# A recommender tower on one core: two transfers moved in the DMA queue of SyncE

## The chip, the core and the metric

The kernel runs on one core of one Trainium2 chip. Its work is spread over five engines with an instruction stream each: TensorE (PE, matmuls into PSUM), VectorE (DVE), ScalarE (ACT), GpSimd (POOL) and SyncE (SP, which here only issues DMAs and waits). They order themselves by semaphores. The metric is the device time of one execution in microseconds; the kernel before takes 625.06 us (median of three runs, 624.83 to 626.06).

## The reference

For 1024 samples, 32 rows of 16 floats are gathered from 32 embedding tables. Three layers follow, in which every feature of the layer before is multiplied with every original row and contracted with weights; the sums over the 16 dimensions go with 16 dense inputs through a top network of three matrices.

```python
def _L0_rec_ref(embeddings, W0, W1, W2):
    x0 = embeddings
    xk = x0
    outs = []
    for W in (W0, W1, W2):
        xk = jax.nn.relu(jnp.einsum('bmd,bhd,mhk->bkd', x0, xk, W))
        outs.append(jnp.sum(xk, axis=2))
    return jnp.concatenate(outs, axis=1)
e = jnp.stack([tbl_0[ids[:, 0]], ...], axis=1)
z = _L0_rec_ref(e, L0_rec_W0, L0_rec_W1, L0_rec_W2)
h = jnp.concatenate([z, dense_ctx], axis=1)
h = jnp.maximum(h @ W_top1 + b_top1, 0.0)
h = jnp.maximum(h @ W_top2 + b_top2, 0.0)
y = h @ W_top3
```

## The kernel before, in words

The 1024 samples are worked in 16 steps of 64 samples; a step is 1024 columns (64 samples x 16 dimensions) wide. All in f32. Steps are numbered from 0 here, so "step 1" is the second.

A step's data goes through these stages:

1. **Gather.** POOL issues 16 indirect DMAs (line 291) that bring the step's rows into `emb` (two buffers, even and odd steps). The gathers of steps 0 and 1 stand at POOL's start; those of step s + 2 are spread behind POOL's six products of step s (1, 1 and 8 behind the three of layer 1, then 1, 1 and 4 behind the three of layer 2).
2. **Store.** When the last of them has landed, SP stores `emb` to a scratch tensor in HBM, `x0_rows` (`store_rows`, line 236, two DMAs, 192 KB).
3. **Load.** When the store has landed, SP loads `x0g` (`load_x0g`, line 246, 512 KB) and then sixteen tiles `x0bc` (`load_tiles`, line 263, 512 KB each). The tiles live in a ring of 24 slots, so the first eight of a step can be loaded early and the other eight wait until tiles of the step before have been used in its layer 2.
4. **Layers.** DVE multiplies pairs of tiles with the layer's input (line 336), PE contracts the products with weights (line 518). Layer 0 uses tiles 0 to 3 in two DVE instructions; layers 1 and 2 use all sixteen, of which DVE takes tiles 0 to 12 in eight instructions (seven groups, the first in two halves) and POOL tiles 13 to 15 (line 306; 11 to 15 or 12 to 15 in the last two steps). POOL's tile k of a layer goes to PE before DVE's group 2, 3 and 5. DVE's products have a ring of 4, POOL's too.
5. **ACT** moves PE's result to the next layer's input for DVE (`x_ps`, line 418) and for POOL (`x_sb`, line 435), and makes the layer sums.

On DVE and PE the order is: layer 1 of step s, layer 0 of step s + 1, layer 2 of step s. The weights of the top network (seven DMAs on SP, line 278: 256, 160, 512 and 64 KB and three of 1 or 2 KB) are first waited for by PE in step 4. Arrivals of tiles are counted by one semaphore per pair of tiles (`bc_in[g]`), so a reader of tile 14 waits for tile 15 as well.

What sets the order around the change is the order of SP's program: SP issues strictly in turn, and a wait holds all that stands behind it. `x0bc` of step 0 is issued without a wait, and then SP waits for the gathers of step 1.

Of the kernel before, what the change touches and what calls it, by code (L numbers as in the profile page):

```python
# [27 lines left out]
STEPS = len(ROWS_OF)  # L28
FIRST_ROW = [sum(ROWS_OF[:s]) for s in range(STEPS + 1)]
QUART = P // FIELDS  # L30
GATHERS_OF = [n // QUART for n in ROWS_OF]
GATHERS = max(GATHERS_OF)
TILES = FIELDS * MAPS // P
# [6 lines left out]
GROUP = 2  # L40
# [8 lines left out]
POOL_COUNT = [POOL_OF.get(s, (3, 3)) for s in range(STEPS)]  # L49
POOL_BEFORE = {0: [], 3: [2, 3, 5], 4: [2, 3, 4, 5], 5: [2, 3, 4, 5, 5]}  # L50
GATHERS_AFTER = {1: [1, 1, 8], 2: [1, 1, 4]}


def columns(s):

    return slice(DIM * FIRST_ROW[s], DIM * FIRST_ROW[s + 1])


def width(s):
    return DIM * ROWS_OF[s]  # L60
# [7 lines left out]
def pool_tiles(s, l):  # L68
    return list(range(TILES - POOL_COUNT[s][l - 1], TILES)) if l else []
# [12 lines left out]
def before(x):  # L82

    return sum(len(groups_of(*y)) for y in STAGES[:NUMBER[x]])
# [6 lines left out]
def pool_before(x):  # L91

    return sum(len(pool_tiles(*y)) for y in STAGES[:NUMBER[x]])
# [46 lines left out]
    return FIRST_ROW[min(s + 1, LAST)] // 2 + (1 if s == LAST else 0)  # L140


def slot(s, j):
    return (TILES * s + j) % SLOTS


def cin_tower_kernel(nc, table, ids, id_offset, dense_t, w0_a, w0_b, w0_sq, w1, w2,
                     wt1_a, wt1_b, bt1, wt2, bt2, wt3, x0_rows, out):
    with ExitStack() as ctx:
        def sb(name, shape, dt=F32):  # L150
            return ctx.enter_context(nc.sbuf_tensor(name, shape, dt))
# [4 lines left out]
        def sem(name):  # L156
            return ctx.enter_context(nc.semaphore(name))
# [10 lines left out]
        x0bc = sb("x0bc", [P, SLOTS, PAIR])  # L168
# [34 lines left out]
        gathered = [sem(f"gathered{i}") for i in range(2)]  # L203
        scratch_out = [sem(f"scratch_out{i}") for i in range(2)]
        x0g_in = sem("x0g_in")
        bc_in = [sem(f"bc_in{g}") for g in range(TILES // GROUP)]
        w0_ready = sem("w0_ready")
        x0g_placed = sem("x0g_placed")
        squared = sem("squared")
# [6 lines left out]
        copied = [sem(f"copied{l}") for l in range(2)]  # L216
# [13 lines left out]
        @block.sync  # L230
        def _(sp):
            def store_rows(s):
                turn, cols = s % 2, columns(s)
                sp.wait_ge(gathered[turn], 16 * sum(GATHERS_OF[turn:s + 1:2]))
                for a, b in ((0, FIELDS), (FIELDS, X0_ROWS)):
                    sp.dma_start(x0_rows[a:b, cols].rearrange("f (q c) -> f q c", q=QUART),  # L236
                                 emb[0:QUART * (b - a), turn, 0:DIM * GATHERS_OF[s]]).then_inc(scratch_out[turn], 16)

            def load_x0g(s):
                if s > 0:  # L240

                    sp.wait_ge(x0g_placed, s)
                    sp.wait_ge(squared, s)
                rows = bass.AP(x0_rows.tensor, DIM * FIRST_ROW[s],
                               [[COLS, FIELDS], [QUART * COLS, QUART], [1, width(s)]])
                sp.dma_start(x0g[:, 0:width(s)], rows).then_inc(x0g_in, 16)  # L246

            def wait_free(k):

                s, j = divmod(k, TILES)  # L250
                if j in pool_tiles(s, 2):
                    sp.wait_ge(pool_products, pool_before((s, 2)) + pool_tiles(s, 2).index(j) + 1)
                else:
                    sp.wait_ge(products, before((s, 2)) + j // GROUP + 1)

            def load_tiles(s):
                for j in range(TILES):
                    k = TILES * s + j
                    if k >= SLOTS:
                        wait_free(k - SLOTS)  # L260
                    rows = x0_rows[SHIFT[j]:SHIFT[j] + FIELDS, columns(s)].unsqueeze(1).to_broadcast(
                        [FIELDS, QUART, width(s)])
                    sp.dma_start(x0bc[:, slot(s, j), 0:width(s)], rows).then_inc(bc_in[j // GROUP], 16)  # L263

            sp.dma_start(ids_sb[:], ids).then_inc(ids_in, 16)
            sp.dma_start(off_sb[:], id_offset).then_inc(ids_in, 16)
            for dst, src in ((w0a_in, w0_a), (w0b_in, w0_b), (wsq_in, w0_sq), (w1_sb[:], w1), (w2_sb[:], w2)):
                sp.dma_start(dst, src).then_inc(weights_in, 16)

            for s in range(STEPS):  # L270
                store_rows(s)
                sp.wait_ge(scratch_out[s % 2], 32 * (s // 2 + 1))
                load_x0g(s)
                load_tiles(s)
                if s == 1:
                    for dst, src in ((wt1a_sb[:], wt1_a), (wt1b_sb[:], wt1_b), (wt2_sb[:], wt2), (wt3_sb[:], wt3),
                                     (bt1_sb[:], bt1), (bt2_sb[:], bt2), (zt_b[MAPS:, :], dense_t)):
                        sp.dma_start(dst, src).then_inc(mlp_in, 16)

            sp.wait_ge(stored, 16 * len(CHUNKS))  # L280

        @block.gpsimd
        def _(pool):
            def gather(s, a, b):
                turn = s % 2
                if a == 0 and s >= 2:

                    pool.wait_ge(scratch_out[turn], 32 * (s // 2))
                for n in range(a, b):
                    at = FIRST_ROW[s] // QUART + n  # L290
                    pool.indirect_dma_start(emb[:, turn, DIM * n:DIM * (n + 1)], None, table,  # L291
                                            bass.IndirectOffsetOnAxis(row_sb[:, at:at + 1], 0)
                                            ).then_inc(gathered[turn], 16)

            def layer(s, l, x):
                if not pool_tiles(s, l):
                    return
                gathers = GATHERS_AFTER[l]
                done = 0 if l == 1 else sum(GATHERS_AFTER[1])
                pool.wait_ge(copied[l - 1], 4 * (s + 1))  # L300
                for k, j in enumerate(pool_tiles(s, l)):
                    pool.wait_ge(bc_in[j // GROUP], 32 * (s + 1))
                    n = pool_before((s, l)) + k
                    if n >= POOL_RING:
                        pool.wait_ge(pool_products_used, n - POOL_RING + 1)
                    pool.tensor_tensor(pool_prod[:, n % POOL_RING, 0:width(s)], x0bc[:, slot(s, j), 0:width(s)],  # L306
                                       x[:, 0:width(s)], ALU.mult).then_inc(pool_products, 1)
                    if s + 2 < STEPS:
                        gather(s + 2, done, done + gathers[k])
                        done += gathers[k]  # L310

            pool.wait_ge(ids_in, 32)
            for cols in (slice(0, GATHERS_OF[0]), slice(GATHERS_OF[0], BATCH // QUART)):
                pool.tensor_tensor(row_sb[:, cols], ids_sb[:, cols],
                                   off_sb[:].to_broadcast([P, cols.stop - cols.start]), ALU.add).then_inc(rows_done, 1)
            pool.wait_ge(rows_done, 1)
            gather(0, 0, GATHERS_OF[0])
            pool.wait_ge(rows_done, 2)
            gather(1, 0, GATHERS_OF[1])
            pool.wait_ge(w0_ready, 2)  # L320
            for s in range(STEPS):
                layer(s, 1, x1_sb)
                layer(s, 2, x2_sb)

        @block.vector
        def _(dve):
# [13 lines left out]
            def layer0(s):  # L340
                dve.wait_ge(x0g_placed, s + 1)
                for g, group in enumerate(groups_of(s, 0)):
                    dve.wait_ge(bc_in[g], 32 * (s + 1))
                    product(s, before((s, 0)) + g, group, x0g_ps)

            def layer(s, l, x):
                for g, group in enumerate(groups_of(s, l)):
                    if l == 1:
                        dve.wait_ge(bc_in[g], 32 * (s + 1))
                    n = before((s, l)) + g  # L350
                    if g == 0:

                        for h in range(2):
                            dve.wait_ge(spread_done[l - 1], 4 * s + 2 * h + 2)
                            product(s, n, group, x, h)
                    else:
                        product(s, n, group, x)
# [35 lines left out]
        def _(act):  # L393
# [16 lines left out]
            def finish(s, l, x=None, x_sb=None):  # L410
# [17 lines left out]
                if s > 0 and l < 2:  # L428
                    act.wait_ge(summed[l], s)
                act.activation(relu[:, l, 0:half(s)], ps[:, 0:half(s)], ACT.Relu).then_inc(relu_done[l], 1)  # L430
                if x is not None:
                    act.wait_ge(relu_done[l], s + 1)
                    for h in range(2):
                        for copy in range(2):
                            act.activation(x_sb[MAPS * copy:MAPS * (copy + 1), half(s) * h:half(s) * (h + 1)],  # L435
                                           relu[MAPS * h:MAPS * (h + 1), l, 0:half(s)], ACT.Copy
                                           ).then_inc(copied[l], 1)
# [238 lines left out]
```

## Time and profile before

| | |
|---|---|
| time, median of 3 runs | 625.06 us (624.83 to 626.06) |
| profiled execution | 622.48 us, of which the span of the profile is 620.7 us |
| PE busy | 563.6 us, 91% |
| DVE busy | 546.5 us, 88% |
| POOL busy | 488.3 us, 79% |
| ACT busy | 308.2 us, 50% |
| DMA | 150.89 MB, mean 243 GB/s |
| mean granted clock of TensorE | 0.991 |

A timeline row gives the start in us from the span's start, the time taken, the engine and line, the instruction with its output and inputs, how often it was repeated in the row, and in brackets the idle time of its engine before it and what ended this. Several instructions in a row without idle time are merged into one. In a table of windows, each engine has its busy time and the number of its instructions in the stretch; the last three columns are the granted clock, the busy share of the 16 DMA engines and what they moved.

### The profile page before, as it was taken

How to read it: one execution, taken by the hardware profiler on the slowest of the kernel's cores; microseconds unless marked ns; L12 is line 12 of the kernel's file. 1: busy time of each engine (PE TensorE's matmuls, PEld its weight loads, DVE VectorE, ACT ScalarE, POOL GpSimd, SP SyncE). 2: the span in 40 equal slices, each digit the busy share in tenths (PEclk: the TensorE clock that was granted, in tenths of full speed). 3: DMA queues.
4: the chain of work that ended last, by engine and by line, in shares of the span. 5: the costliest groups of instructions: out<-in, count | busy, mean ns of one | idle time of the engine just before them, and what ended most of it. 6: DMA issues, size and time to landing. Idle time of an engine off the chain costs nothing.

```text
span 620.7 us, 7817 instructions
## 1 busy us (share of the span) xinstructions
PE 563.6 (91%) x2548; PEld 194.8 (31%) x2548; DVE 546.5 (88%) x321; ACT 308.2 (50%) x1345; POOL 488.3 (79%) x364
## 2 busy tenths in 40 slices
PE   0058997999999999999999999999999999999997
PEld 0012232332322333333333333333333333334354
DVE  0038997999999999999999999999999999999580
ACT  0023735355464745455476736454565736454442
POOL 6765888887889798988888788988888797949360
PEclk9997999999999999999999999999999999999998
DMA  3198878778586868788686858787776858687000
GB/s 99 29 375 315 309 249 310 274 267 295 191 314 210 316 218 311 270 299 295 223 289 215 310 199 313 261 310 274 251 275 213 289 212 311 255 306 271 2 1 0
DMA packets 52852, 150.89 MB, mean 243 GB/s; under 512 B 9830, under 2 KB 17386, under 8 KB 52810
## 3 DMA queue, kind: packets, MB, share of 16 engines
q1 hardware_dynamic: 44608, 148.27, 65.6%
q0 software_dynamic: 8192, 2.11, 2.5%
q8 instruction: 20, 0.33, 0.2%
q14 instruction: 22, 0.18, 0.1%
q10 hardware_dynamic: 10, 0.00, 0.0%
HBM read 147.20 MB, written 3.15 MB: 242 GB/s over the span
## 4 chain that ended last, share of the span: by engine, by line
DVE 33%; PE 29%; DMA 19%; issue 8%; POOL 8%; SPq 2%; ACT 1%; DVEq 0%; POOLq 0%
DVE prod L336 31%; PE y_ps L518 26%; DMA x0bc<-x_rows 14%; POOL emb L291 6%; DMA emb<-table,row_sb 2%; DVE z L364 2%; DMA x_rows<-emb 2%; PE x0g_ps L579 2%; POOL pool_prod L306 2%; SPq L263 1%; PE x0g_ps L584 1%; PE x0g_ps L602 0%; SPq L236 0%; SPq L246 0%; DMA off_sb<-id_offset 0%
## 5 line engine op out<-in xcount | busy, mean ns | idle before, releaser
L336 DVE TENSOR_TENSOR prod<-x0bc,x_ps 128x2048 f32<-128x2048 f32 (+1 forms) x252 | 456.5, 1887 | 13.6 <-ACT x_ps L418 13.1
L518 PE MATMUL y_ps<-prod,w_sb 128*64 128x512 f32 x1640 | 381.2, 598 | 12.2 <-DVE prod L336 12.0
L291 POOL DMA_INDIRECT emb<-table,row_sb x256 | 244.9, 957 | 65.5 <-issue 62.8
L306 POOL TENSOR_TENSOR pool_prod<-x0bc,x_sb 128x1024 f32<-128x1024 f32 x102 | 242.4, 2384 | 48.1 <-ACT x_sb L435 35.0
L518 PEld LDWEIGHTS y_ps<-prod,w_sb 128*64 128x64 f32 x1640 | 115.5, 137 | 253.4 <-issue 214.0
L425 ACT ACTIVATE relu<-y_ps 128x16 f32<-128x16 f32 x480 | 79.6, 296 | 115.3 <-PE y_ps L518 115.3
L418 ACT ACTIVATE x_ps<-y_ps 64x512 f32<-64x512 f32 x128 | 73.0, 570 | 75.4 <-PE y_ps L518 72.8
L518 PE MATMUL y_ps<-pool_prod,w_sb 128*64 128x512 f32 x408 | 104.9, 594 | 2.1 <-POOL pool_prod L306 2.0
L336 DVE TENSOR_TENSOR prod<-x0bc,x0g_ps 128x2048 f32<-128x2048 f32 x32 | 72.8, 2288 | 37.5 <-DMA x0bc<-x_rows 32.4
L435 ACT ACTIVATE x_sb<-relu 64x512 f32<-64x512 f32 x128 | 80.4, 628 | 3.4
L425 ACT ACTIVATION_READ_ACCUMULATOR relu<-y_ps 128x1 f32 x480 | 79.7, 322 | 0.0
L518 PE MATMUL y_ps<-prod,w0s_sb 128*64 128x512 f32 x256 | 61.2, 616 | 4.0 <-DVE prod L336 4.0
L402 ACT ACTIVATE x0g_ps<-x0g 128x1024 f32<-128x1024 f32 x16 | 16.4, 1028 | 82.0 <-DMA x0g<-x_rows 82.0
L518 PE MATMUL y_ps<-squares,wsq_sb 128*64 128x512 f32 x64 | 17.4, 623 | 35.4 <-ACT squares L408 35.4
L518 PEld LDWEIGHTS y_ps<-pool_prod,w_sb 128*64 128x64 f32 x408 | 28.4, 137 | 61.3 <-issue 47.2
L518 PEld LDWEIGHTS y_ps<-prod,w0s_sb 128*64 128x64 f32 x256 | 18.1, 141 | 45.6 <-issue 28.8
L364 DVE TENSOR_REDUCE z<-relu 128x32 f32<-128x512 f32 x33 | 22.5, 683 | 7.4 <-ACT relu L430 7.4
L430 ACT ACTIVATE relu<-y_ps 128x512 f32<-128x512 f32 x33 | 19.7, 597 | 4.5 <-PE y_ps L518 3.7
L518 PEld LDWEIGHTS y_ps<-squares,wsq_sb 128*64 128x64 f32 x64 | 4.6, 141 | 44.0 <-issue 44.0
L408 ACT ACTIVATE squares<-x0g 128x1024 f32<-128x1024 f32 x16 | 16.7, 1041 | 0.0
L579 PE MATMUL x0g_ps<-h,wt_sb 128*128 128x256 f32 (+1 forms) x64 | 14.6, 376 | 0.0
L579 PEld LDWEIGHTS x0g_ps<-h,wt_sb 128*128 128x128 f32 x64 | 11.3, 190 | 5.8 <-issue 4.1
(34 smaller groups left out, 71.0 us busy)
## 6 DMA issues: line engine op xcount, KB each, us to landing
x0bc<-x_rows SPq DMA_DIRECT2D x256, 512.0 KB, 7.0
x0g<-x_rows SPq DMA_DIRECT2D x16, 512.0 KB, 4.7
emb<-table,row_sb POOLq DMA_INDIRECT x256
x_rows<-emb SPq DMA_DIRECT2D x16, 128.0 KB, 2.1
w_sb<-w SPq DMA_DIRECT2D x2, 512.0 KB, 4.7
x_rows<-emb SPq DMA_DIRECT2D x16, 64.0 KB, 2.0
wt_sb<-wt SPq DMA_DIRECT2D x1, 512.0 KB
wt1a_sb<-wt_a SPq DMA_DIRECT2D x1, 256.0 KB
```

Of the source, the lines that this page charges most:

```text
L291: pool.indirect_dma_start(emb[:, turn, DIM * n:DIM * (n + 1)], None, table, bass.IndirectOffsetOnAxis(row_sb[:, at:at + 1], 0)).then_inc(g ...
L306: pool.tensor_tensor(pool_prod[:, n % POOL_RING, 0:width(s)], x0bc[:, slot(s, j), 0:width(s)], x[:, 0:width(s)], ALU.mult).then_inc(pool_p ...
L336: made = dve.tensor_tensor(out, left, right, ALU.mult)
L364: dve.tensor_reduce(z[:, l, FIRST_ROW[s] // 2:FIRST_ROW[s + 1] // 2], relu[:, l, 0:half(s)].rearrange("p (b d) -> p b d", d=DIM), AX_X, AL ...
L402: act.activation(x0g_ps[:, :, 0:half(s)], x0g[:, 0:width(s)].rearrange("p (h c) -> p h c", h=2), ACT.Copy).then_inc(x0g_placed, 1)
L408: act.activation(squares[:, 0:width(s)], x0g[:, 0:width(s)], ACT.Square).then_inc(squared, 1)
L418: act.activation(x[MAPS * copy:MAPS * (copy + 1), h, 0:half(s)], ps[MAPS * h:MAPS * (h + 1), 0:half(s)], ACT.Relu).then_inc(spread_done[l], 1)
L425: act.activation(relu[:, l, cols], ps[:, cols], ACT.Relu, accum_out=z[:, l, at:at + 1]).then_inc(relu_done[l], 1)
L430: act.activation(relu[:, l, 0:half(s)], ps[:, 0:half(s)], ACT.Relu).then_inc(relu_done[l], 1)
L435: act.activation(x_sb[MAPS * copy:MAPS * (copy + 1), half(s) * h:half(s) * (h + 1)], relu[MAPS * h:MAPS * (h + 1), l, 0:half(s)], ACT.Copy ...
L518: made = pe.matmul(ps[MAPS * h:MAPS * (h + 1), 0:half(s)], w, moving[:, half(s) * h:half(s) * (h + 1)], start=first, stop=final)
L579: made = pe.matmul(x0g_ps[:, j, 0:n], wt2_sb[:, k, P * j:P * (j + 1)], h1[:, k, 0:n], start=k == 0, stop=k == H1_TILES - 1)
```

## The change

The helper `load_tiles` gets two positions from a table, `AHEAD = {0: (14, 16)}`. In step 0 the store of step 1's rows (with its wait for the gathers) is issued before tile 14 instead of behind tile 15; `load_x0g(1)` stays behind tile 15. In the other steps both stay behind the tiles. The wait for the store goes into `load_x0g`. The top network's weights are loaded at `s == 3` instead of `s == 1`. As `load_tiles(s)` now ends with the store and the `x0g` load of step s + 1, the weights stand between `x0g` of step 4 and the tiles of step 4, where before they stood between the tiles of step 1 and the store of step 2. `bc_in` is split into even and odd steps. `GATHERED_FIRST = 2` leaves the gathers as they are, and `copies_after` gives the same counts as before, since every step has POOL tiles.

```diff
+GATHERED_FIRST = 2
+AHEAD = {0: (14, 16)}
...
             def load_x0g(s):
+                sp.wait_ge(scratch_out[s % 2], 32 * (s // 2 + 1))
                 if s > 0:
...
             def load_tiles(s):
-                for j in range(TILES):
+                store_at, load_at = AHEAD.get(s, (TILES, TILES))
+                for j in range(TILES + 1):
+                    if s + 1 < STEPS:
+                        if j == store_at:
+                            store_rows(s + 1)
+                        if j == load_at:
+                            load_x0g(s + 1)
+                    if j == TILES:
+                        break
...
-                    sp.dma_start(x0bc[:, slot(s, j), 0:width(s)], rows).then_inc(bc_in[j // GROUP], 16)
+                    sp.dma_start(x0bc[:, slot(s, j), 0:width(s)], rows).then_inc(bc_in[s % 2][j // GROUP], 16)
...
+            store_rows(0)
+            load_x0g(0)
             for s in range(STEPS):
-                store_rows(s)
-                sp.wait_ge(scratch_out[s % 2], 32 * (s // 2 + 1))
-                load_x0g(s)
                 load_tiles(s)
-                if s == 1:
+                if s == 3:
                     for dst, src in ((wt1a_sb[:], wt1_a), (wt1b_sb[:], wt1_b), (wt2_sb[:], wt2), (wt3_sb[:], wt3),
...
-                pool.wait_ge(copied[l - 1], 4 * (s + 1))
+                pool.wait_ge(copied[l - 1], copies_after(s, l - 1))
...
-                    pool.wait_ge(bc_in[j // GROUP], 32 * (s + 1))
+                    pool.wait_ge(bc_in[s % 2][j // GROUP], 32 * (s // 2 + 1))
```

The first place is SP's queue at the end of step 0. Before (a number behind an x is how many equal instructions stand there; the first row is `x0g` of step 0, the last the tiles of step 1):

```order
L246 DMA x0g<-x_rows 128x1x1024 [waits scratch_out0]
L263 DMA x0bc<-x_rows 128x1x1024 x16
L236 DMA x_rows<-emb 32x4x256 [waits gathered1]
L236 DMA x_rows<-emb 16x4x256
L246 DMA x0g<-x_rows 128x1x1024 [waits squared,x0g_placed,scratch_out1]
L263 DMA x0bc<-x_rows 128x1x1024 x8
```

And now, where the lines are 257 for `x0g`, 282 for the tiles and 246 for the store:

```order
L257 DMA x0g<-x_rows 128x1x1024 [waits scratch_out0]
L282 DMA x0bc<-x_rows 128x1x1024 x14
L246 DMA x_rows<-emb 32x4x256 [waits gathered1]
L246 DMA x_rows<-emb 16x4x256
L282 DMA x0bc<-x_rows 128x1x1024 x2
L257 DMA x0g<-x_rows 128x1x1024 [waits squared,x0g_placed,scratch_out1]
L282 DMA x0bc<-x_rows 128x1x1024 x8
```

The store of step 1 has passed tiles 14 and 15 of step 0.

The second place is SP's queue around the top network's weights (`wt`, `bt` and `zt_b`). Before, from the last eight tiles of step 1 to the first tiles of step 2:

```order
L263 DMA x0bc<-x_rows 128x1x1024 [waits products] x8
L278 DMA wt1a_sb<-wt_a 128x512
L278 DMA wt1b_sb<-wt_b 80x512
L278 DMA wt_sb<-wt 128x1024
L278 DMA wt_sb<-wt 128x2
L278 DMA bt_sb<-bt 128x4
L278 DMA bt_sb<-bt 128x2
L278 DMA zt_b<-dense_t 16x1024
L236 DMA x_rows<-emb 32x4x256 [waits gathered0]
L236 DMA x_rows<-emb 16x4x256
L246 DMA x0g<-x_rows 128x1x1024 [waits squared,x0g_placed,scratch_out0]
L263 DMA x0bc<-x_rows 128x1x1024 [waits products] x5
```

Now, from the last eight tiles of step 3 to the first tiles of step 4:

```order
L282 DMA x0bc<-x_rows 128x1x1024 [waits products] x8
L246 DMA x_rows<-emb 32x4x256 [waits gathered0]
L246 DMA x_rows<-emb 16x4x256
L257 DMA x0g<-x_rows 128x1x1024 [waits squared,x0g_placed,scratch_out0]
L296 DMA wt1a_sb<-wt_a 128x512
L296 DMA wt1b_sb<-wt_b 80x512
L296 DMA wt_sb<-wt 128x1024
L296 DMA wt_sb<-wt 128x2
L296 DMA bt_sb<-bt 128x4
L296 DMA bt_sb<-bt 128x2
L296 DMA zt_b<-dense_t 16x1024
L282 DMA x0bc<-x_rows 128x1x1024 [waits products] x5
```

The seven loads have gone from ahead of a store to between an `x0g` load and the tiles of the same step.

## Rows read from the trace of the kernel before

**Rows 1.** Windows of the whole core: a stretch of steps 4 to 8, four single microseconds

```profile
175.00:307.00 132.00, 129.51 (x590) 44.09 (x592) 132.00 (x78) 74.03 (x343) 113.97 (x84) 1.00 0.75 265
...
55.00:56.00 1.00, 1.00 (x6) 0.38 (x8) 1.00 (x1) 0.00 (x0) 0.98 (x2) 1.00 0.00 0
...
87.00:88.00 1.00, 0.88 (x6) 0.16 (x4) 1.00 (x2) 1.00 (x16) 1.00 (x1) 1.00 0.79 191
88.00:89.00 1.00, 1.00 (x6) 0.32 (x6) 1.00 (x1) 1.00 (x16) 0.84 (x1) 1.00 0.07 16
...
122.00:123.00 1.00, 0.98 (x6) 0.10 (x2) 1.00 (x2) 0.00 (x0) 1.00 (x1) 1.00 0.24 84
```

**Rows 2.** Timeline of DVE: layer 0 of steps 1, 2, 3 and 4

```profile
62.81 2.29 DVE L336 TENSOR_TENSOR prod<-x0bc,x0g_ps 128x2048 f32<-128x2048 f32 x1 [2.66 <-DMA x0bc<-x_rows]
65.47 2.29 DVE L336 TENSOR_TENSOR prod<-x0bc,x0g_ps 128x2048 f32<-128x2048 f32 x1 [0.37 <-DMA x0bc<-x_rows]
...
100.73 2.29 DVE L336 TENSOR_TENSOR prod<-x0bc,x0g_ps 128x2048 f32<-128x2048 f32 x1 [3.02 <-issue]
...
135.50 4.48 DVE L336 TENSOR_TENSOR prod<-x0bc,x0g_ps 128x2048 f32<-128x2048 f32 x2
...
155.47 14.47 DVE L336 TENSOR_TENSOR prod<-x0bc,x_ps 128x1024 f32<-128x1024 f32 x8
169.99 2.29 DVE L336 TENSOR_TENSOR prod<-x0bc,x0g_ps 128x2048 f32<-128x2048 f32 x1
172.53 2.29 DVE L336 TENSOR_TENSOR prod<-x0bc,x0g_ps 128x2048 f32<-128x2048 f32 x1 [0.26 <-DMA x0bc<-x_rows]
```

**Rows 3.** Timeline of SP's DMA issues

```profile
48.95 1.21 SPq L236 DMA_DIRECT2D x_rows<-emb  x2
55.39 0.55 SPq L246 DMA_DIRECT2D x0g<-x_rows  x1
...
78.44 0.60 SPq L278 DMA_DIRECT2D wt1a_sb<-wt_a  x1
...
81.59 0.45 SPq L278 DMA_DIRECT2D zt_b<-dense_t  x1
89.99 1.22 SPq L236 DMA_DIRECT2D x_rows<-emb  x2
...
123.75 1.21 SPq L236 DMA_DIRECT2D x_rows<-emb  x2
...
159.99 1.21 SPq L236 DMA_DIRECT2D x_rows<-emb  x2
...
163.24 22.24 SPq L263 DMA_DIRECT2D x0bc<-x_rows  x16
```

**Rows 4.** Timeline of POOL: products (L306) and last gathers (L291) of steps

```profile
52.48 2.36 POOL L306 TENSOR_TENSOR pool_prod<-x0bc,x_sb 128x1024 f32<-128x1024 f32 x1 [8.29 <-DMA x0bc<-x_rows]
...
56.00 2.38 POOL L306 TENSOR_TENSOR pool_prod<-x0bc,x_sb 128x1024 f32<-128x1024 f32 x1
...
85.50 0.94 POOL L291 DMA_INDIRECT emb<-table,row_sb  x1 [0.30 <-issue]
...
119.48 0.94 POOL L291 DMA_INDIRECT emb<-table,row_sb  x1 [0.30 <-issue]
...
143.68 2.37 POOL L306 TENSOR_TENSOR pool_prod<-x0bc,x_sb 128x1024 f32<-128x1024 f32 x1 [3.29 <-ACT x_sb L435]
...
157.08 0.95 POOL L291 DMA_INDIRECT emb<-table,row_sb  x1 [0.30 <-issue]
```

**Rows 5.** Chain of waits: start us, us, what (gather and store landings)

```profile
43.25 5.68 DMA emb<-table,row_sb
...
49.55 5.82 DMA x_rows<-emb
...
191.41 2.58 DMA emb<-table,row_sb
...
226.25 2.24 DMA emb<-table,row_sb
```

More of the change, by code:

```diff
@@ L140, in summed2_after, with copies_after @@
     return FIRST_ROW[min(s + 1, LAST)] // 2 + (1 if s == LAST else 0)
+def copies_after(s, l):
+    return 4 * sum(1 for i in range(s + 1) if pool_tiles(i, l + 1))
 def slot(s, j):
@@ L205, in cin_tower_kernel @@
         x0g_in = sem("x0g_in")
-        bc_in = [sem(f"bc_in{g}") for g in range(TILES // GROUP)]
+        bc_in = [[sem(f"bc_in{i}_{g}") for g in range(TILES // GROUP)] for i in range(2)]
         w0_ready = sem("w0_ready")
@@ L307, in layer @@
                                        x[:, 0:width(s)], ALU.mult).then_inc(pool_products, 1)
-                    if s + 2 < STEPS:
+                    if GATHERED_FIRST <= s + 2 < STEPS:
                         gather(s + 2, done, done + gathers[k])
@@ L318, in _ @@
             pool.wait_ge(rows_done, 2)
-            gather(1, 0, GATHERS_OF[1])
+            for s in range(1, GATHERED_FIRST):
+                gather(s, 0, GATHERS_OF[s])
             pool.wait_ge(w0_ready, 2)
@@ L342, in layer0 @@
                 for g, group in enumerate(groups_of(s, 0)):
-                    dve.wait_ge(bc_in[g], 32 * (s + 1))
+                    dve.wait_ge(bc_in[s % 2][g], 32 * (s // 2 + 1))
                     product(s, before((s, 0)) + g, group, x0g_ps)
@@ L348, in layer @@
                     if l == 1:
-                        dve.wait_ge(bc_in[g], 32 * (s + 1))
+                        dve.wait_ge(bc_in[s % 2][g], 32 * (s // 2 + 1))
                     n = before((s, l)) + g
@@ L430, in finish @@
                 act.activation(relu[:, l, 0:half(s)], ps[:, 0:half(s)], ACT.Relu).then_inc(relu_done[l], 1)
-                if x is not None:
+                if x is not None and pool_tiles(s, l + 1):
                     act.wait_ge(relu_done[l], s + 1)
```

## The prediction

> **What bounds the kernel now.** I read the windows first, for the engine that never rests; then DVE's timeline, for the places where it does rest; then back from each rest to the DMA that ended it, through SP's timeline and POOL's. From 175 to 307 us DVE is busy 132.00 of 132.00 us and PE 129.51 [rows 1]: from step 4 on a step is as long as DVE's work for it, and a shift of DVE there moves all that follows. The early rests stand in DVE's timeline [rows 2]. Layer 0 of step 1 starts at 62.81 after 2.66 us idle and waits 0.37 more for tiles 2 and 3. Layer 0 of step 2 starts at 100.73 after 3.02 us idle. The view says "issue" there, but the only input that comes just then is the pair of tiles, as in the other steps. In step 3 (135.50) there is no wait. In step 4 DVE comes free at 155.47 + 14.47 = 169.94, starts at 169.99, and waits 0.26 more at 172.53. So the tiles of step 4 arrive as DVE wants them, with no slack.
>
> Each wait ends a chain: POOL's last gather of the step, its landing, store, `x0g`, tiles. For step 2 the last gather starts at 85.50 [rows 4] and the store at 89.99 [rows 3], 10.74 us ahead of DVE's start. In step 4: 157.08, 159.99, and 10.00 us to 169.99.
>
> **Part 1, the store of step 1 ahead of tile 14.** The gathers of step 1 have landed at 43.25 + 5.68 = 48.93, and SP stores at 48.95 in both kernels [rows 3, 5]. Today the store waits in the queue behind all sixteen tiles: its second DMA takes 5.82 us. At 55 to 56 us the DMA engines are then empty, 0.00 busy [rows 1], since `x0g` is only issued at 55.39. Now the store has two tiles fewer in front. A pair of tiles takes 172.53 - 169.99 = 2.54 us [rows 2], so the store lands near 52.8, and tiles 14 and 15, about as late as today, fill the hole. Step 1's tiles come some 2.6 us earlier and take away most of the 2.66 us of DVE's wait at 62.81 (not all: PE, half a product behind, must free a slot of DVE's ring of products first; I guess a start near 61).
>
> What is late next? POOL. It starts the product of tile 13 at 52.48, when tiles 12 and 13 land, which are ahead of the moved store and land as before. The product of tile 14 starts at 56.00 and needs tile 15. Tile 15 now has the store in front, but all bytes together are the same and were through the engines before 55 us [rows 1], so it is in time by about half a microsecond. PE therefore ends layer 1 of step 0 when it does today, since it takes POOL's products in between. ACT's inputs for layer 2 follow, so DVE can use only a part of what it gained (it would be through with layer 0 ahead of them), and POOL none: from ACT's copy on POOL works without rest to its gather at 85.50. The gathers of step 2 do not move. I cost part 1 at 0 at the end: between -0.3 us, which is the one issue gap in that stretch of POOL [rows 4], and +0.5 us, if tile 15 is that much too late for POOL and delays all its gathers.
>
> **Part 2a, the weights leave step 1.** Seven issues, from 78.44 to 81.59 + 0.45 = 82.04, take 3.6 us of SP [rows 3]. That is hidden: SP waits until 89.99 for gathers. Not hidden is the transfer. It is 256 + 160 + 512 + 64 KB and some small ones, 995 KB, against 1024 KB in 2.54 us for a pair of tiles: 2.5 us, behind the tiles of step 1. The DMA engines are busy until 88 us and empty from 88 to 89 [rows 1]. The gather of 85.50 has landed at 89.99, 4.49 us after its start. Gathers issued when the queue has just drained take 2.58 and 2.24 us [rows 5], in step 4 2.91 (159.99 - 157.08). Without the weights the queue drains at about 85.5, and the gather lands after 2.2 to 2.9 us. Gain at the store of step 2: 4.49 - 2.6 = 1.9 us (1.6 to 2.2). DVE waits 3.02 us at 100.73, and more by what it gained in part 1, so all of the 1.9 is taken: DVE starts layer 0 of step 2 1.9 us earlier.
>
> Does it survive until step 4? For step 3 POOL's last gather at 119.48 cannot move, as its run of products and gathers starts from ACT's copy of layer 1 of step 1, which rests on unmoved work of PE and POOL. It lands today at 123.73, after 4.25 us, behind tiles that drain at 122.3 (0.24 busy in 122 to 123 [rows 1]). With the tiles of step 2 1.9 us earlier it lands after 2.6 to 2.9, so the store moves from 123.75 to about 122.2, 1.5 us. DVE at 135.50 had no wait and I take half a microsecond of slack, so nearly all of the 1.9 stays. For step 4 POOL waits 3.29 us at 143.68 for ACT [rows 4]; this is the point where POOL takes over the shift from DVE and PE. Its gather at 157.08, the store at 159.99 and `x0g` of step 4 are 1.9 us earlier.
>
> The Trainium skill has a rule that speaks against this gain: in "DMA: Bandwidth & Descriptors", section "Queues, rings and completion order", each DMA engine takes turns between the queues at packet granularity, so a gather on its own queue would not wait for what SP's queue holds. The rows above speak against it, 4.2 to 5.7 us with tiles in the queue and 2.2 to 2.9 without; by the rule the gain would be 0 and the end 2.6 us later than today. That result is rival C.
>
> **Part 2b, the weights stand in step 4.** They are issued between `x0g` and the first tile, on the one path that has no slack. Two bounds. By bytes, 2.5 us, if SP keeps the queue full (they need 995/1024 of a pair's 2.54 us). By SP, the first tile is issued 3.6 us later [rows 3], and if the queue then runs empty all 3.6 show. Below, nothing is hidden unless the weights pass in the hole between the `x0g` issue and its data; then the cost could fall toward 0. I take 2.6 us, near the bytes: the three big loads carry 928 KB, some 2.3 us of work for the DMA engines, and the four small issues behind them take SP 4 x 0.45 = 1.8 us [rows 3], so the queue should just about stay fed. From step 4 on DVE has no rest to hide it. SP's own waits behind (the ring's slots, the store of step 5) get later by less, and POOL's gathers of step 5 are not touched. PE needs the weights after layer 0 of step 5, past 205 us, long after they land, in both kernels.
>
> **The sum**, on the profiled execution (span 620.7, whole 622.48 us): part 1 0, part 2a -1.9, part 2b +2.6, together +0.7, so 623.2. The median of the runs is 625.06, and with +0.7 it is 625.8 us.
>
> **Edits with no cost.** The split semaphores and the new counts add no instruction to DVE, ACT or POOL and change no wait's moment. The gathers stay.
>
> **Rivals.**
> - A, slower: SP's issue time decides at step 4, not the bytes. The small loads (1 to 64 KB) take 0.45 us each to issue and move little, so the queue runs dry and the tiles come 3.6 us later: -1.9 + 3.6 = +1.7, 626.8 us. It decides where `x0g` and the three big loads are through before the first tile's data starts. For it speaks that the DMA engines move only 191 GB/s in the last microsecond of the weights today [rows 1].
> - B, faster: the weights cost little in step 4, as they pass while `x0g` of step 4 is still starting, and the gains remain: -1.9 + 0.4 = -1.5, 623.6 us. Against it: today's tiles of step 4 follow at the pace of bytes, one pair in 2.54 us, so the hole is already used by tiles.
> - C, slower: the gather's landing is not what the weights delay, so step 2 starts as today and the 2.6 of step 4 is paid in full: 627.7 us.
> - That the kernel doesn't do what it says is excluded by the order of SP's queue; that part 1's 2.6 us reach the end (622.5 us) would need POOL's gathers of step 2 to move, and I give it no chance of its own.
>
> **How the numbers follow.** Forecast (+0.1 to +1.4, 625.2 to 626.5, from 1.6 to 2.2 against 2.3 to 3.0) 0.52; A 0.19; B 0.17; C 0.12. A difference under 0.2%, 1.25 us here, is about what a measurement of this kernel cannot tell from none: faster is below 623.8, slower above 626.3. Faster: most of B, 0.15. Slower: C, most of A, the upper edge of the forecast, 0.31. Same: the rest, 0.54. The range takes in A and reaches to B and C: 623.6 to 627.5.
>
> **What would show it.** In the profile after: the store of step 1 lands near 53 and the DMA engines are busy through 55 to 56 us; DVE's layer 0 of step 1 near 61; POOL's product at 56.0 unmoved; POOL's last gather of step 2 still at 85.5 but the store at 88; DVE's layer 0 of step 2 at 98.8; the stores of steps 3 and 4 at 122.2 and 158.1; DVE's layer 0 of step 4 at 170.7 after some 2.7 us of idle time; and from there a constant shift of +0.7. It is wrong if POOL's product of tile 14 starts after 56.5, if the store of step 2 stays near 90, or if DVE idles under 1.5 or over 3.5 us at step 4.

## The result, and the profile after

| | before | changed |
|---|---|---|
| median of 20 runs | 624.45 us | 626.91 us |
| lowest and highest | 622.71 to 626.22 | 624.32 to 631.25 |
| profiled execution | 622.48 us | 627.61 us |

The ratio is 1.0036, with a 95% interval from 1.0022 to 1.0049: the change makes the kernel 2.3 us slower (1.4 to 3.1). Ratios, here and below, are taken without the executions that were over 1.5% slower than the fastest of their kernel; the medians take them in. The time lies in the stated range (623.6 to 627.5) and on the forecast's side of no change, but the move is three times the +0.7 us of its sum.

SP's issues in the changed kernel (line 246 is the store, 257 `x0g`, 282 the tiles, 296 the weights), against [rows 3]:

```profile
48.71 1.21 SPq L246 DMA_DIRECT2D x_rows<-emb  x2
49.96 1.24 SPq L282 DMA_DIRECT2D x0bc<-x_rows  x2
52.80 0.51 SPq L257 DMA_DIRECT2D x0g<-x_rows  x1
...
87.83 1.21 SPq L246 DMA_DIRECT2D x_rows<-emb  x2
...
122.43 1.21 SPq L246 DMA_DIRECT2D x_rows<-emb  x2
...
157.88 1.21 SPq L246 DMA_DIRECT2D x_rows<-emb  x2
160.51 0.57 SPq L257 DMA_DIRECT2D x0g<-x_rows  x1
161.12 0.59 SPq L296 DMA_DIRECT2D wt1a_sb<-wt_a  x1
...
164.19 0.43 SPq L296 DMA_DIRECT2D zt_b<-dense_t  x1
164.66 23.20 SPq L282 DMA_DIRECT2D x0bc<-x_rows  x16
```

`x0g` of step 1 goes out at 52.80 where it was 55.39, and the stores of steps 2, 3 and 4 are 2.2, 1.3 and 2.1 us earlier than before. The weights push the first tile of step 4 to 164.66.

DVE's layer 0 of steps 1 to 4, against [rows 2]:

```profile
61.41 4.49 DVE L355 TENSOR_TENSOR prod<-x0bc,x0g_ps 128x2048 f32<-128x2048 f32 x2 [1.43 <-PE y_ps L537]
...
97.89 2.29 DVE L355 TENSOR_TENSOR prod<-x0bc,x0g_ps 128x2048 f32<-128x2048 f32 x1 [0.73 <-issue]
101.85 2.29 DVE L355 TENSOR_TENSOR prod<-x0bc,x0g_ps 128x2048 f32<-128x2048 f32 x1 [1.68 <-DMA x0bc<-x_rows]
...
134.01 4.61 DVE L355 TENSOR_TENSOR prod<-x0bc,x0g_ps 128x2048 f32<-128x2048 f32 x2
...
171.85 2.29 DVE L355 TENSOR_TENSOR prod<-x0bc,x0g_ps 128x2048 f32<-128x2048 f32 x1 [3.29 <-issue]
174.89 2.29 DVE L355 TENSOR_TENSOR prod<-x0bc,x0g_ps 128x2048 f32<-128x2048 f32 x1 [0.75 <-DMA x0bc<-x_rows]
```

Most of the story can be read here. At 134.01 DVE is 1.5 us ahead of the kernel before (135.50). In step 4 it rests 3.29 + 0.75 = 4.04 us, where it rested 0.05 + 0.26 = 0.31. Afterwards it stands at 174.89 against 172.53: 2.36 us behind, close to the difference of the medians (2.46).

POOL, against [rows 4]:

```profile
52.49 2.35 POOL L324 TENSOR_TENSOR pool_prod<-x0bc,x_sb 128x1024 f32<-128x1024 f32 x1 [8.44 <-DMA x0bc<-x_rows]
...
56.03 2.38 POOL L324 TENSOR_TENSOR pool_prod<-x0bc,x_sb 128x1024 f32<-128x1024 f32 x1
...
85.53 0.94 POOL L309 DMA_INDIRECT emb<-table,row_sb  x1 [0.30 <-issue]
...
142.18 2.37 POOL L324 TENSOR_TENSOR pool_prod<-x0bc,x_sb 128x1024 f32<-128x1024 f32 x1 [2.34 <-ACT x_sb L454]
...
155.58 0.94 POOL L309 DMA_INDIRECT emb<-table,row_sb  x1 [0.30 <-issue]
```

POOL's product of tile 14 starts at 56.03 (56.00 before) and its last gather of step 2 at 85.53 (85.50): the first edit passes POOL by. The gather of 85.53 has landed by 87.83, when SP starts the store, 2.30 us later, where it took 4.49. At 142.18 POOL takes over the shift.

Windows of the changed kernel, with the granted clock, the busy share of the DMA engines and GB/s as the last three columns:

```profile
55.00:56.00 1.00, 1.00 (x6) 0.38 (x8) 1.00 (x1) 0.00 (x0) 0.98 (x1) 1.00 0.84 295
88.00:89.00 1.00, 1.00 (x8) 0.37 (x6) 1.00 (x1) 1.00 (x16) 0.87 (x1) 1.00 0.00 0
165.00:166.00 1.00, 1.00 (x6) 0.28 (x4) 1.00 (x2) 1.00 (x2) 1.00 (x1) 1.00 1.00 303
166.00:167.00 1.00, 1.00 (x8) 0.39 (x6) 1.00 (x1) 0.89 (x1) 0.84 (x2) 1.00 1.10 336
167.00:168.00 1.00, 1.00 (x8) 0.33 (x6) 1.00 (x2) 0.00 (x0) 0.70 (x2) 1.00 1.10 210
168.00:169.00 1.00, 1.00 (x6) 0.29 (x4) 0.56 (x1) 0.00 (x0) 0.69 (x2) 1.00 0.95 328
```

The hole at 55 us is filled (0.84 busy, 0.00 before). Around the weights, from 165 to 169, the engines are full all the time but move 210 to 336 GB/s: what passes is slow, and the queue does not run dry.

### The profile page after: what moved, and what is told of

The parts are those of the page before. It is cut to its first block, busy times and chain, and to the rows that moved or that the text cites. A ratio compares the mean times of both kernels' runs of the same rounds, so it can differ in the third digit from the quotient of the medians.

```text
span 625.8 us, 7817 instructions
## 1 busy us (share of the span) xinstructions
PE 562.4 (90%) x2548; PEld 195.1 (31%) x2548; DVE 546.7 (87%) x321; ACT 308.3 (49%) x1345; POOL 488.2 (78%) x364
## 4 chain that ended last, share of the span: by engine, by line
PE 34%; DVE 31%; DMA 19%; issue 8%; POOL 4%; SPq 3%; ACT 1%; DVEq 0%; POOLq 0%
PE y_ps L537 30%; DVE prod L355 29%; DMA x0bc<-x_rows 17%; POOL emb L309 3%; SPq L282 3%; PE x0g_ps L598 2%; DVE z L383 2%; POOL pool_prod L324 1%; DMA emb<-table,row_sb 1%; DMA x_rows<-emb 1%; PE x0g_ps L621 1%; PE x0g_ps L603 1%; ACT x_ps L437 0%; DMA off_sb<-id_offset 0%; SPq L246 0%
```

## The experiments

Two theories. **S**: the first edit is worth nothing at the end; taking the weights out of step 1 gains 1.4 us or more at step 2; putting them ahead of the tiles of step 4 costs 4 us there. **T**: the loss is in the first edit or in something after step 4, and the weights' place is of no account. The runs were made in three groups, each on a chip of its own, with runs of the kernel before between them. The chips differ by several us, so times are compared within a group or by the ratio to the kernel before.

| run | group | median us | before | ratio (95%) |
|---|---|---|---|---|
| e1_start | 1 | 625.63 | 629.27 | 0.9948 (0.9921 to 0.9976) |
| e2_ahead_only | 1 | 627.79 | 629.27 | 0.9979 (0.9953 to 1.0004) |
| e3_weights_only | 1 | 630.83 | 629.27 | 1.0034 (1.0007 to 1.0061) |
| e4_big_here | 1 | 628.58 | 629.27 | 0.9996 (0.9969 to 1.0022) |
| e6_start_no_ahead | 2 | 627.07 | 628.68 | 0.9977 (0.9947 to 1.0007) |
| e1_start_again | 2 | 625.98 | 628.68 | 0.9949 (0.9921 to 0.9977) |
| e8_behind_tile3 | 2 | 624.45 | 628.68 | 0.9927 (0.9898 to 0.9957) |
| c_after | 2 | 631.01 | 628.68 | 1.0026 (0.9995 to 1.0057) |
| e7_before_store4 | 3 | 626.25 | 624.99 | 1.0014 (0.9996 to 1.0033) |
| e5_small_here | 3 | 626.06 | 624.99 | 1.0013 (0.9996 to 1.0031) |
| e2_ahead_again | 3 | 625.31 | 624.99 | 1.0005 (0.9986 to 1.0024) |
| c_before | 3 | 624.2, one run | 624.99 | |

All experiments start from the changed kernel, and share a helper that issues a list of the seven loads:

```diff
+            big, small = weights[:3], weights[3:]
+            def load_weights(which):
+                for dst, src in which:
+                    sp.dma_start(dst, src).then_inc(mlp_in, 16)
```

**e1_start and e1_start_again: the weights at the program's start.**

```diff
+            load_weights(weights)
             store_rows(0)
             load_x0g(0)
             for s in range(STEPS):
                 load_tiles(s)
-                if s == 3:
...
```

> As the changed kernel, but the top network's seven weight loads are issued at the program's start, behind w1 and w2, where the DMA queue and SP have nothing else to do until the first store. Theory S (the changed kernel lost its time because the weights stand ahead of the tiles of step 4, some 4 us there, and had gained 1.4 to 1.5 us at step 2 by their absence from step 1): DVE's layer 0 of step 4 has no long wait (under 0.5 us), its sum of step 3 (the row at 177.09 in the changed kernel) comes near 173.2, and the kernel is 1.2 to 2.0 us faster than before, ratio 0.997 to 0.998. Rival T (the loss lies in the first edit or in a slow drift after step 4, not in the weights' place): still 1 us or more slower than before, ratio above 1.001.

> e1_start once more, beside its counterpart without the first edit and beside the changed kernel. Theory S: 1.5 to 3 us faster than before (0.995 to 0.9975) and 4 to 5 us faster than the changed kernel.

0.9948 and 0.9949: about 3.3 us faster than before in both groups, and 5.0 us faster than the changed kernel beside it. T falls: with the same first edit, only the weights' place has changed the sign. The gain is above what I expected of the first run (1.2 to 2.0 us), of which only the upper part lies in its interval; where the rest comes from, the profiles do not show. The long wait is gone in the first profile; the second still has 1.85 us, as its last gather took 3.5 us to land (157.58 to 161.11), which I did not expect and cannot explain.

**e2_ahead_only and e2_ahead_again: the first edit alone.**

```diff
                     if s + 1 < STEPS:
+                        if j == TILES and s == 1:
+                            load_weights(weights)
                         if j == store_at:
                             store_rows(s + 1)
```

> The first edit alone: the store of step 1 ahead of tile 14 of step 0, and the weights back between the tiles of step 1 and the store of step 2. Theory S: step 1 starts about 1.4 us earlier on DVE (61.4), but POOL's gathers of step 2 stay at 85.5 and the store at 89.9, so nothing is left of it: ratio 0.9995 to 1.0005. Rival T: the first edit has a sign of its own, 1 us or more either way (0.998 or 1.002).

> The first edit alone once more, since its first ratio, 0.9979 with an interval from 0.9953 to 1.0004, left open whether it is worth anything. Theory S: 0.999 to 1.001. Rival T: 0.998 or less.

0.9979 and 1.0005, both with 1 in their intervals; the first lies outside what I expected (0.9995 to 1.0005), the second inside (0.999 to 1.001). In the second profile the store of step 2 is where it was:

```profile
90.29 1.21 SPq L246 DMA_DIRECT2D x_rows<-emb  x2
```

and DVE waits at 100.42 as before:

```profile
100.42 2.29 DVE L361 TENSOR_TENSOR prod<-x0bc,x0g_ps 128x2048 f32<-128x2048 f32 x1 [2.57 <-issue]
```

What the first edit gains in step 1 DVE spends waiting in step 2. A worth of 1 us at the end is not excluded by the times; the traces show no way for it.

**e6_start_no_ahead: weights at the start, the first edit undone** (`AHEAD = {}`).

> Weights at the program's start, and the store of step 1 behind all tiles of step 0 as before: e1_start without the first edit. Theory S (the first edit is worth nothing at the end, since POOL's gathers of step 2 do not move): within 0.1% of e1_start on the same chip, both 1.5 to 3 us faster than before. Rival T (the first edit is worth 1 us or more, as e2_ahead_only at 0.9979 hints): 1 to 2 us slower than e1_start.

627.07 beside 625.98 us for e1_start_again: 1.1 us apart, with intervals that overlap widely. The 0.1% of theory S was missed (the ratios are 0.28% apart), and T's 1 us fits. But the run is inconclusive: its interval allows no effect as well as 1 us.

**e3_weights_only: the second edit alone** (`AHEAD = {}`, weights at `s == 3`).

> The second edit alone: the weights ahead of the tiles of step 4, and the store of step 1 behind all tiles of step 0 as before. Theory S: as the changed kernel, ratio 1.003 to 1.004, store of step 2 near 88, DVE idle near 4 us in layer 0 of step 4. Rival T: the second edit is about free and this runs like before (0.999 to 1.001).

1.0034, like the changed kernel's 1.0036 and 1.0026. The second edit alone makes a loss of that size. DVE rests 5.23 + 0.49 us in layer 0 of step 4.

**e4_big_here and e5_small_here: which of the seven loads cost.** In e4 the small four are at the start, in e5 the big three:

```diff
+            load_weights(small)
             store_rows(0)
             load_x0g(0)
...
                 if s == 3:
+                    load_weights(big)
...
```

> As the changed kernel, but only the three big weight loads (928 KB) stand ahead of the tiles of step 4; the three of 1 or 2 KB and the dense inputs are loaded at the program's start. It parts the cost of 4 us by what is moved. If the bytes make the cost (2.5 us for all 995 KB), DVE waits 2.3 to 2.6 us there and the kernel is about 1 us slower than before (1.001 to 1.002). If the small loads' many short pieces and their issue time make the rest, the same 2.3 to 2.6 us is seen here and the missing 1.5 us is theirs. If the small loads cost nothing, DVE waits 4 us as in the changed kernel and the ratio is 1.0035.

> Only the four small loads (67 KB together, in pieces of 8 bytes to 4 KB) stand ahead of the tiles of step 4, the three big ones are at the program's start. With e4_big_here (DVE idle 4.8 us there against 5.7 in e3_weights_only and 4.0 in the changed kernel) the two should add up. If the cost follows the bytes, DVE waits under 0.5 us here; if it follows SP's issue time (4 x 0.45 = 1.8 us), 1.8 us. I expect 0.9 to 1.2 us less the 0.3 us that DVE waits there anyway, and a kernel 0.5 to 2 us faster than before (0.997 to 0.999).

DVE's layer 0 of step 4, first e4 (its store is at 164.53), then e5 (store at 158.33):

```profile
177.59 2.29 DVE L362 TENSOR_TENSOR prod<-x0bc,x0g_ps 128x2048 f32<-128x2048 f32 x1 [4.09 <-issue]
180.56 2.29 DVE L362 TENSOR_TENSOR prod<-x0bc,x0g_ps 128x2048 f32<-128x2048 f32 x1 [0.69 <-DMA x0bc<-x_rows]
```

```profile
169.73 2.29 DVE L362 TENSOR_TENSOR prod<-x0bc,x0g_ps 128x2048 f32<-128x2048 f32 x1 [0.93 <-issue]
172.47 2.29 DVE L362 TENSOR_TENSOR prod<-x0bc,x0g_ps 128x2048 f32<-128x2048 f32 x1 [0.45 <-DMA x0bc<-x_rows]
```

DVE's idle time depends on when it came free. Free of that is the time from the store of step 4 to the start of DVE's first pair, wherever DVE had to wait for it:

| between `x0g` and tile 0 | store to pair 0, us | more than without (mean 10.3) |
|---|---|---|
| nothing (before, c_before, e2_ahead_only, e6, e1_start_again, e7) | 10.0, 10.3, 10.3, 10.5, 10.3, 10.2 | |
| all seven, 995 KB (changed, c_after, e3) | 14.0, 14.1, 14.0 | 3.8 |
| big three, 928 KB (e4) | 13.1 | 2.8 |
| small four, 67 KB (e5) | 11.4 | 1.1 |

The two add up to the whole, 2.8 + 1.1 = 3.9 against 3.8, but each is one profile, and the six without loads differ by 0.5 among themselves. The big loads take 2.8 us where tiles of the same bytes take 2.3. For the small four, 1.0 to 1.1 us stands against 0.2 by their bytes and 1.8 by their issue on SP. What e5 alone does not settle is whether their transfer or their issue makes it. Its windows:

```profile
164.00:165.00 1.00, 1.00 (x7) 0.29 (x5) 1.00 (x1) 0.00 (x0) 1.00 (x1) 1.00 0.96 217
165.00:166.00 1.00, 1.00 (x8) 0.42 (x6) 1.00 (x2) 0.56 (x1) 1.00 (x1) 1.00 0.85 130
166.00:167.00 1.00, 1.00 (x8) 0.29 (x4) 1.00 (x1) 1.00 (x2) 0.84 (x2) 1.00 0.86 337
```

The kernel before, where `x0g` is issued at 162.63 and its data start at 164:

```profile
164.00:165.00 1.00, 1.00 (x8) 0.43 (x6) 1.00 (x2) 0.00 (x0) 0.87 (x1) 1.00 0.88 135
165.00:166.00 1.00, 1.00 (x8) 0.29 (x4) 1.00 (x1) 0.00 (x0) 0.98 (x2) 1.00 0.81 303
```

The first microsecond of a transfer into an empty queue looks there (0.88 busy, 135 GB/s) like the row at 165 in e5 (0.85, 130). SP issues tile 0 in e5 at 163.62, 5.29 us after the store instead of 3.25; with the same 1.4 us from issue to data as above it would start at 165.0. So in e5 SP's issue time, rival A's cause, explains the 1.1 us as well as slow pieces do. In the changed kernel it does not: there tile 0, issued at 164.66, could start near 166, but from 162 to 167 the engines move 127 + 358 + 383 + 303 + 336 = 1507 KB, which is `x0g` and the weights (512 + 995), so that tile 0 starts near 167 by this estimate. e8 below shows the weights' transfer with SP far ahead of it. The Trainium skill says in "DMA: Bandwidth & Descriptors", section "Rules for kernel authors", that under 64 KB one pays mostly overhead; three of the four loads (1 or 2 KB, in pieces of 8 or 16 bytes per partition) are under it, and the fourth, sixteen rows of 4 KB, is at it. The times agree with it: the changed kernel's 3.8 us less e4's 2.8 leave 1.0 us for 67 KB. The expected ratio of e5 (0.997 to 0.999) was missed, at 1.0013 (0.9996 to 1.0031); that of e4 (1.001 to 1.002) too, at 0.9996. e4's expectation lies inside its interval, e5's just outside; the profiles, not the times, carry this reading.

**e7_before_store4: the weights in step 3, but ahead of the store of step 4.**

```diff
+                        if j == TILES and s == 3:
+                            load_weights(weights)
                         if j == store_at:
                             store_rows(s + 1)
```

> The weights at the end of step 3, but ahead of the store of step 4 instead of behind its x0g load: the same place in step 3 that they had in step 1 in the kernel before; the first edit is on. SP's issue time is hidden there, as SP waits for gathers. Theory S: the last gather of step 4 lands 1 to 1.9 us later, as it did in step 2, DVE waits 1 to 2 us in layer 0 of step 4, no 4 us, and the time is that of the kernel before (0.998 to 1.001). Rival (the step matters, not the place in SP's queue): as the changed kernel, 1.0035.

SP's issues, POOL's last gather of step 4, and DVE:

```profile
149.08 0.64 SPq L292 DMA_DIRECT2D wt1a_sb<-wt_a  x1
...
152.22 0.44 SPq L292 DMA_DIRECT2D zt_b<-dense_t  x1
161.34 1.22 SPq L246 DMA_DIRECT2D x_rows<-emb  x2
```

```profile
155.50 0.95 POOL L315 DMA_INDIRECT emb<-table,row_sb  x1 [0.30 <-issue]
```

```profile
171.53 2.29 DVE L361 TENSOR_TENSOR prod<-x0bc,x0g_ps 128x2048 f32<-128x2048 f32 x1 [3.19 <-issue]
```

The gather takes 161.34 - 155.50 = 5.84 us to land instead of 2.30. I had expected 1 to 1.9 us of delay and 1 to 2 us of waiting; it was 3.5 and 3.2 (and 0.44 for the second pair). So this place is about as bad in the profile, 3.6 us, as the one ahead of the tiles; the ratio of 1.0014 cannot tell it from either. The rival, that the step and not the place in SP's queue matters, is refuted by the next run.

**e8_behind_tile3: the weights in step 4, behind its tile 3.**

```diff
                     k = TILES * s + j
+                    if s == 4 and j == 4:
+                        load_weights(weights)
```

> The changed kernel with the seven weight loads four tiles later, between tiles 3 and 4 of step 4, so that layer 0 of step 4 has its tiles first. Theory S has two costs in the changed kernel: DVE's wait of 4.0 us in layer 0 of step 4, and behind it POOL's wait of 1.5 us for tiles 12 and 13 of step 4, which makes a gather late and shows as a wait of DVE in step 6. Here DVE's wait in step 4 is under 0.6 us, and the kernel is faster than before by 1 us or more (0.996 to 0.999), unless POOL's wait stays and costs 0.5 to 1 us in step 6. Rival: what costs is not the place ahead of tile 0 but the extra 995 KB in step 4 anywhere, then it is as slow as the changed kernel (1.002 or more).

SP's issues and DVE's layer 0 of step 4:

```profile
159.40 1.21 SPq L246 DMA_DIRECT2D x_rows<-emb  x2
162.02 0.56 SPq L257 DMA_DIRECT2D x0g<-x_rows  x1
162.63 2.61 SPq L284 DMA_DIRECT2D x0bc<-x_rows  x4
165.29 0.65 SPq L292 DMA_DIRECT2D wt1a_sb<-wt_a  x1
...
169.18 16.05 SPq L284 DMA_DIRECT2D x0bc<-x_rows  x12
```

```profile
169.84 4.57 DVE L361 TENSOR_TENSOR prod<-x0bc,x0g_ps 128x2048 f32<-128x2048 f32 x2
```

The same seven loads take about the same SP time (3.85 us from 165.29 on, 3.50 us in the changed kernel), in the same step, and DVE does not wait: both pairs of tiles are there, and tiles 4 to 15 are not wanted until layer 1. The windows in which the weights pass:

```profile
172.00:173.00 1.00, 1.00 (x8) 0.30 (x6) 0.99 (x2) 0.64 (x2) 0.70 (x2) 1.00 1.14 285
173.00:174.00 1.00, 1.00 (x8) 0.41 (x6) 1.00 (x1) 0.98 (x2) 0.69 (x2) 1.00 0.99 288
174.00:175.00 1.00, 1.00 (x7) 0.28 (x4) 1.00 (x3) 0.95 (x3) 0.91 (x1) 1.00 1.16 256
175.00:176.00 1.00, 1.00 (x8) 0.29 (x4) 1.00 (x2) 0.94 (x3) 0.79 (x1) 1.00 0.96 283
```

SP had issued all seven by 169.14 and the next tile at 169.18, so its issue time cannot matter here. Still the engines move only 256 to 288 GB/s at full load, where tiles move 392 in the microsecond before. These 1112 KB would have taken 2.8 us at that pace and took 4, so the weights cost 1.2 us beyond the 2.5 us of their bytes: 3.6 to 3.7 us, an estimate from these rows that agrees with the 3.8 of the table. The price is the transfer's; at this place DVE does not pay it.

The ratio is 0.9927 (0.9898 to 0.9957), 4.6 us faster than before by it and 6.6 us faster than the changed kernel beside it by the medians. I had expected 0.996 to 0.999. It is the fastest version that I ran and beats both kernels. Against e1_start_again, 1.5 us slower, the intervals overlap. The second cost that I had named, POOL's wait for tiles 12 and 13 of step 4 (1.49 us in the changed kernel), is absent here too. It goes with the place ahead of tile 0; whether it costs anything of its own is not shown. Nor do the profiles show where the 3.3 and 4.6 us of e1_start and e8 come from in full: the gains that I can read in the traces are 1.5 to 2 us, which is within the interval of the two e1 runs and below that of e8 (2.7 to 6.4 us).

**c_after and c_before: both kernels once more.**

> The changed kernel itself, on the same chip as these, to see how its profile varies from one execution to the next. Its idle time of DVE in layer 0 of step 4 is again 3.5 to 4.5 us, ratio 1.002 to 1.005.

> The kernel before itself, for a second profile of it: which of its waits move from one execution to the next. The wait in layer 0 of step 2 is again near 3.4 us and that of step 4 under 0.6 us, whatever the granted clock does near 50 us.

As expected: 3.60 + 0.42 us in layer 0 of step 4 of the changed kernel, 0.22 + 0.23 us in that of the kernel before, which waits 3.23 + 0.67 us in layer 0 of step 2. The ratio of c_after, 1.0026, has 1 just inside its interval (0.9995); the run beside the result, 1.0036, has it outside.

## Why the prediction was right, and where it was off

The measured 626.91 us lies in the stated range because that takes in rival A (626.8); it is above the forecast's own 625.2 to 626.5. By the boundary of 1.25 us the change is slower, which had 0.31, and not the same, which had 0.54. DVE's idle time at step 4, 4.04 us, is also beyond the 3.5 us that the prediction named as a sign of being wrong. So the place in the range is partly luck.

- **Part 1 at 0: right.** The store landed at 52.8 as forecast, DVE's layer 0 of step 1 began at 61.41 (61), POOL's products did not move by 0.1 us, and two runs of this edit alone gave 0.9979 and 1.0005. What it brings in step 1 is lost in step 2. That it is exactly 0 the times do not show.
- **Part 2a, -1.9 us: right in mechanism and nearly in size.** The store of step 2 moved by 2.16 us (89.99 to 87.83, forecast 88), those of steps 3 and 4 to 122.43 and 157.88 (122.2 and 158.1). DVE started layer 0 of step 2 at 97.89, even earlier than 98.8, but tiles 2 and 3 came 3.96 us behind tiles 0 and 1 instead of 2.6, so that 1.5 us were left at 134.01. Between e7_before_store4 and e2_ahead_again, which differ up to there by the weights alone, the stores of step 2 are at 88.05 and 90.29, and layer 0 of step 3 is 133.91 and 135.96, 2.05 us apart. Rival C, with no such gain, is refuted, and with it what the prediction drew from the rule of the Trainium skill ("DMA: Bandwidth & Descriptors", section "Queues, rings and completion order") on queues that take turns, namely that a gather would not wait for what SP's queue holds: it took 4.49 and 5.84 us behind tiles and weights against 2.30. Whether the queues take turns packet by packet, no run shows.
- **Part 2b, +2.6 us: the step that was mis-sized.** It measured 3.8 us to the first pair, by the time from the store, on the mean of three profiles against six, and DVE's idle time in layer 0 grew by 3.7 us (4.04 against 0.31). "I take 2.6 us, near the bytes" took the weights at the pace of tiles. The experiments put 2.8 us on the big three (2.3 by bytes), and 1.0 us is left for the small four, which I had at nearly nothing because SP's issue of them is hidden behind the big ones. It is hidden; their transfer is not. That the seven together pass below the pace of tiles is shown with SP far ahead (e8); the split between big and small rests on single profiles. Rival A had almost the right number (3.6) from the wrong cause: it wanted the queue to run dry, and the engines were 0.95 to 1.10 busy from 165 to 169. The prediction also had POOL's gathers of step 5 untouched. The last of them starts at 190.01 in the changed kernel and the store at 195.95, 5.94 us later, where it was 2.60 (191.41 to 194.01); DVE's layer 0 of step 5 still has no wait (207.04).
- **The sum**, on DVE: it is free for step 4 at 168.56 (171.85 - 3.29) where it was 169.94, 1.4 us early, and then rests 3.7 us more. That makes +2.4 in place of +0.7; the profile shows +2.36 at tiles 2 and 3 of step 4, the medians +2.46. Behind that point a shift of DVE stays, as forecast.
- **Open.** The two profiled executions of the result differ by 5.1 us, not 2.4. Some 1.7 us more arise between step 4 and DVE's last long wait, in small waits for tiles, and 1.0 us behind DVE's last instruction, a stretch that differs as much between any two profiles (6.9 and 7.9 us, 7.9 and 6.3 in c_before and c_after). The first stretch took 418.8 us before and 420.5 after (418.5 and 420.9 in c_before and c_after), and 418.8 to 422.4 in the experiments. All four profiles with the big loads ahead of tile 0 are at 420.5 or above (e3 421.4, e4 422.4), but so are e1_start_again (420.5) and e6 (421.9), so a late cost of that place is neither shown nor excluded. The medians do not ask for it. Why the last gather of e1_start_again took 3.5 us to land ahead of step 4, with the queue drained, stays unexplained too. It is not alone: e2_ahead_only has 3.53 us and e4 3.79 us at the same place. In all three the store comes right behind POOL's next gather (161.10 and 161.11, 164.49 and 164.52, 164.25 and 164.53), which is a hint and not a cause.

The lines of the last point, DVE's wait for the last step's layer 2 in the kernel before and in the changed one:

```profile
591.30 9.01 DVE L336 TENSOR_TENSOR prod<-x0bc,x_ps 128x1024 f32<-128x1024 f32 x5 [8.64 <-ACT x_ps L418]
```

```profile
595.37 6.81 DVE L355 TENSOR_TENSOR prod<-x0bc,x_ps 128x1024 f32<-128x1024 f32 x4 [8.64 <-ACT x_ps L437]
```

## What to carry to other kernels

A bulk load that nobody wants yet belongs behind the transfers that someone waits for, not merely into a later step: the same seven loads held the tiles back by 3.8 us ahead of tile 0 and by 3.5 us ahead of a store whose gathers must land first, and made no long wait of DVE behind tile 3 or at the program's start. Before a transfer is moved, read what stands behind it in its queue and who waits for that. And price small loads by the time in which the DMA engines are busy and move little, not by their bytes.

## What the runs showed of the hardware

A busy share of 1 says nothing of the pace: seven weight loads passed at 256 to 288 GB/s with the DMA engines 0.96 to 1.16 busy, where 512 KB tiles moved 392. The 67 KB of the small four (pieces of 8 and 16 bytes and rows of 4 KB) account for 1.0 us. A gather's landing depends on what is in SP's queue: 2.30 us with it drained, 4.49 to 5.94 us with it full.

TensorE's granted clock fell in thirteen of the fourteen profiles for some microseconds near 50 us, with different starts and lengths. In the kernel before it was at the lower of its two levels (0.50, 1.2 GHz) from 47 to 53; in the first experiment from 49 to 56 and beyond; in the changed kernel's profile not at all (1.00 in every window from 40 us on). In the first two PE had been idle just before. But so it had in the third (0.28 us busy from 44 to 48), so the idle time alone does not tell them apart. The rows of the kernel before and of e1_start:

```profile
46.00:47.00 1.00, 0.00 (x0) 0.00 (x0) 1.00 (x2) 0.95 (x3) 0.00 (x0) 0.78 1.04 389
47.00:53.00 6.00, 4.91 (x12) 1.48 (x14) 6.00 (x4) 2.90 (x5) 0.52 (x1) 0.50 1.03 406
```

```profile
48.00:49.00 1.00, 0.00 (x0) 0.00 (x0) 0.00 (x0) 0.00 (x0) 0.00 (x0) 0.57 1.06 368
49.00:56.00 7.00, 2.74 (x8) 0.89 (x10) 5.15 (x4) 5.39 (x9) 0.67 (x1) 0.50 1.01 358
```

In e1_start, POOL's first product starts at 55.33 instead of 52.48, since it then waits for ACT's input and not for tile 13. That moves every gather behind it by 2.9 us, more than the whole change is worth. Single profiles of this kernel are compared by distances from a common event, as in the table above, and not by their ends.
